# A one-hot tile built by four Vector comparisons with a per-partition number instead of one comparison of two SBUF operands, beside a stream of GpSimd gathers

## The reference

```python
# twice (cgconv, then relu)
z = concat([x[dst], x[src]], -1)
m = sigmoid(z @ Wf + bf) * softplus(z @ Ws + bs)
x = x + segment_sum(m, dst)
# twice (gat_conv, then batch norm)
alpha = leaky_relu(a_src[src] + a_dst[dst] + a_edge)
p = exp(alpha - segment_max(alpha, dst)[dst]);  p = p / segment_sum(p, dst)[dst]
out = segment_sum((x @ W)[src] * p[:, None], dst) + bias
```

## Time and profile before

| what | value |
|---|---|
| median of 3 runs | 11049.12 us (11041.77 to 11055.13) |
| profiled execution, span from the first to the last instruction | 9392.2 us |
| profiled execution, its own time | not given; the median of the runs is 1656.9 us above the span |
| GpSimd busy | 6571.9 us, 70% of the span |
| TensorE busy (weight loads) | 5120.9 us, 55% (4302.7 us, 46%) |
| Vector busy | 4670.8 us, 50% |
| ScalarE busy | 3046.4 us, 32% |
| gathers L677, L1134 | 3328 each, 985 and 961 ns mean |

### The profile page before, as it was taken

One profiled execution on the slowest core, in us unless ns is written; L12 is line 12 of the kernel. 1 busy time (PEld: TensorE's weight loads), 2 busy tenths in 40 slices (PEclk: granted clock), 3 DMA queues, 4 the chain that ended last, 5 costly groups with the idle time before them and its releaser, 6 DMA issues. The chain is left out here.

```text
span 9392.2 us, 131283 instructions
## 1 busy us (share of the span) xinstructions
PE 5120.9 (55%) x26955; PEld 4302.7 (46%) x26956; DVE 4670.8 (50%) x14160; ACT 3046.4 (32%) x8219; POOL 6571.9 (70%) x6801
## 2 busy tenths in 40 slices
PE   2677777777677777777533253434552234343444
PEld 1555555555555555555423243434542234343443
DVE  6555555555555555555623353434552235353546
ACT  0444444444444444444302122222320122121222
POOL 2777777777577777777557777777716777777771
PEclk6888787788778887887655555555555555555555
DMA  4322223222222232222232232222203223222221
GB/s 134 91 76 77 76 75 76 75 77 77 82 77 77 75 76 77 77 75 76 68 76 53 45 59 50 56 52 52 49 11 75 45 49 59 46 58 49 58 44 30
DMA packets 436755, 612.92 MB, mean 65 GB/s; under 512 B 180134, under 2 KB 217754, under 8 KB 434779
## 3 DMA queue, kind: packets, MB, share of 16 engines
q0 software_dynamic: 214032, 332.71, 17.2%
q1 hardware_dynamic: 217116, 262.20, 10.3%
q10 hardware_dynamic: 5193, 13.44, 0.4%
HBM read 575.04 MB, written 32.78 MB: 65 GB/s over the span
## 5 line engine op out<-in xcount | busy, mean ns | idle before, releaser
L677 POOL DMA_INDIRECT big<-q_table,idx_stage x3328 | 3279.5, 985 | 1007.8 <-issue 930.3
L1134 POOL DMA_INDIRECT big<-xl_table,idx_stage x3328 | 3199.1, 961 | 1007.9 <-issue 985.3
L1405 PE MATMUL bank<-msg,onehot 128*128 128x66 f32 x6656 | 1597.3, 424 | 2227.4 <-DVE wide L1265 2003.0
L1405 PEld LDWEIGHTS bank<-msg,onehot 128*128 128x128 f32 x6656 | 1480.8, 328 | 2276.9 <-issue 2186.1
L774 PE MATMUL bank<-big,ident 128*128 128x512 f32 x1664 | 1216.8, 821 | 1236.0 <-DMA big<-q_table,idx_stage 1145.6
L777 PEld LDWEIGHTS bank<-big,wide 128*128 128x128 f32 x6656 | 1217.7, 257 | 574.9 <-issue 574.9
L777 PE MATMUL bank<-big,wide 128*128 x6656 | 1208.0, 342 | 0.0
L577 DVE TENSOR_TENSOR onehot<-iota,dst_rel 128x512 f32<-128x512 f32 x1664 | 1145.7, 689 | 2.9 <-issue 2.9
L705 DVE SCALAR_TENSOR_TENSOR work<-bank,work 128x256 f32<-128x256 f32 x832 | 352.3, 423 | 1459.7 <-ACT work L747 1456.2
L742 ACT ACTIVATE work<-bank 128x512 f32<-128x512 f32 x832 | 496.2, 596 | 1783.4 <-PE bank L777 1781.1
L1265 DVE TENSOR_TENSOR wide<-wide,bank 128x66 f32 x3328 | 739.4, 222 | 553.8 <-issue 182.6
(11 more groups left out here) (216 smaller groups left out, 4138.3 us busy)
## 6 DMA issues: line engine op xcount, KB each, us to landing
wide<-rel_rows SPq DMA_DIRECT2D x416, 256.0 KB, 3.4
big<-rel_rows SPq DMA_DIRECT2D x416, 256.0 KB
big<-q_table,idx_stage POOLq DMA_INDIRECT x3328
big<-xl_table,idx_stage POOLq DMA_INDIRECT x3328
q_table<-wide SPq DMA_DIRECT2D x12, 1024.0 KB, 5.2
edge_rows<-big SPq DMA_DIRECT2D x25, 257.0 KB, 6.6
xl_table<-big SPq DMA_DIRECT2D x12, 520.0 KB, 6.7
big<-in_edge_attr ACTq DMA_DIRECT2D x6, 1024.0 KB
```

The source lines that it names most:

```text
L677: pool.indirect_dma_start(out=ring[:, u, s % GROUP, :], out_offset=None, in_=k.q_table, in_offset=bass.IndirectOffsetOnAxis(ap=k.idx_stage ...
L1134: pool.indirect_dma_start(out=buf[p][:, s, :], out_offset=None, in_=k.xl_table, in_offset=bass.IndirectOffsetOnAxis(ap=k.idx_stage[:, s:s ...
L1405: last_one = nc.tensor.matmul(sum_bank[c % UNROLL][:, i * P:i * P + C + 2], k.onehot[:, c % UNROLL, i, :], k.msg[:, c % UNROLL, i, 0:C + 2 ...
```

## The change

`build_onehot` writes the same tile. Before, one `tensor_tensor` compares `iota`, repeated four times, with the four numbers of `dst_rel`, each repeated 128 times: 512 elements per partition and two inputs in SBUF. After, four `tensor_scalar` write one step's 128 columns each: one input in SBUF (`iota`) and one [P, 1] scalar per instruction, a column of `dst_rel`. The last of the four increments the semaphore. Both callers keep their place for it.

```diff
 def build_onehot(nc, k, to, s):
 
-    return nc.vector.tensor_tensor(to, k.iota[:, :].unsqueeze(1).broadcast_to([P, GROUP, P]),
-                                   k.dst_rel[:, ds(s, GROUP)].unsqueeze(2).broadcast_to([P, GROUP, P]), ALU.is_equal)
+    for i in range(GROUP):
+        last_one = nc.vector.tensor_scalar(to[:, i, :], k.iota[:, :], k.dst_rel[:, ds(s + i, 1)], None, ALU.is_equal)
+    return last_one
```

## The result

The changed kernel takes 11205.17 us (median of 4 runs, 11199.27 to 11209.2), the kernel before beside it 11045.44 us (4 runs): ratio 1.0144, 95% interval 1.0130 to 1.0158. The forecast was 11011 us and its range ended at 11085. It is slower, by 160 us, where 38 us less were forecast.

What follows compares the result with a forecast made beforehand. GpSimd's 6656 gathers at 1.25 us were taken as the bound, 8320 of 9392 us. Terms -55 (stretch), +16 and +1 (where no gather hides Vector) gave -38: 11049 to 11011 us, range 10955 to 11085.

Steps and rivals of the forecast that it cites:

- If it isn't, it still costs nothing beside gathers: Vector's queue: three more address instructions per group are taken as covered, and otherwise still cost nothing while gathers run.
- no row says what fills it, and I take it as unchanged: Outside the profiled span: the 1657 us between span and median of the runs were taken to stay the same.
- GpSimd never waits for a buffer: GpSimd in the passes: its idle time is nearly all 'issue', so 6656 gathers at 1.25 us set 8320 us.
- wrong in its root: Stated failure condition: stretched gathers end elsewhere than 0.82 us after a comparison's end, or the time outside the span moves.
- stretch by one-hots: Gathers starting inside a one-hot comparison: their stretch falls from 122 to 67 us, a gain of 55 us.
- from the last gather of both attention passes on: After the attention passes' last gathers: Vector's queue sets the pace, 80 groups at 0.20 us more, +16 us.
- the 67 us that were to be left: Gathers beside the four new comparisons: remaining stretch, 10 ns per comparison, 40 ns per group, 67 us in all.
- So each comparison delays only gathers that start in its first 0.286 - 0.125 = 0.161 us: New one-hot comparisons: gathers starting in that window are delayed by 0.08 us on average, 10 ns per comparison.
- The turn within the four: Within a group's four comparisons: a gather goes on at the end of the comparison in which it starts.
- the first rival: Gathers beside the four comparisons get no turn within them: one 0.886 us hold, +195 us, 11244 us; chance 8%, half case 5%.
- Two-port stalls of the writing: Rival, gathers: a two-port comparison also stalls GpSimd's descriptor writing, 11864 us; chance 3%.
- No hold at all: Rival, gathers: the new comparison doesn't hold GpSimd but lasts some 0.335 us, -88 us, 10961 us; chance 10%.

Runs made afterwards that it cites:

- e5: The changed kernel measured again, unaltered, against the kernel before at the upper level: ratio 1.0140.
- e6: The changed kernel with its four comparisons always reading columns 0 to 3 of dst_rel, so no computed addresses, against the kernel before, upper level: 1.0026.
- e16: The changed kernel with dst_rel columns first copied to a small tile and read at fixed places, values kept, against the kernel before, upper level: 1.0042.
- e17: The changed kernel unaltered, measured beside the version with copied columns, against the kernel before at the upper level: 1.0142.
- e7: The kernel before with its one comparison always reading columns 0 to 3 of dst_rel, against the kernel before, upper level: 0.9987.
- e4: The kernel before plus three 128x2 tensor_scalar per group reading a fixed column, against the kernel before, upper level: 1.0064.
- e1: The kernel before, unaltered, profiled once more at the upper level: ratio 0.9994 to the kernel before.
- e12: The changed kernel unaltered, against the kernel before at the lower level: ratio 0.9911.
- e13: The changed kernel with each of its four comparisons as a 128x128 tensor_tensor, against the kernel before, lower level: 0.9943.
- e9: The kernel before with SyncE's rel_rows transfers in the loops filling 16 of 128 partitions, against the kernel before, lower level: 0.9992.
- e8: The kernel before with one comparison of 1024 elements building the one-hots of two groups, against the kernel before, upper level: 1.0030.
- e11: The kernel before with each batch's dst_rel columns copied once to a fixed tile in the attention passes, against the kernel before, lower level: 0.9989.
- e3: The kernel before plus three 128x2 tensor_scalar per group, each with its own computed dst_rel address, against the kernel before, upper level: 1.0110.
- e14: The kernel before plus three 128x2 tensor_scalar per group with computed addresses, against the kernel before, lower level: 1.0160.

## Why the prediction was wrong

**The step that failed at the upper level: "If it isn't, it still costs nothing beside gathers".** It said that the queue's three more address instructions per group either hide or cost nothing, since the gathers set the time. The trace that it was read from had them at 53 to 89 ns. In the runs that were timed many take 0.7 us, single one-hots take several microseconds in place of 0.9, and the gathers wait for buffers. The addresses cost 118 us by the medians of e5 and e6, and again 118 us by those of e16 and e17 (11098.39 - 10980.5; 1.00% by the ratios). The profiled executions say where, in us:

| compared | first passes | attention passes | after their last gathers |
|---|---|---|---|
| addresses: e5 less e6 | +4 | +98 | +14 |
| addresses: e17 less e16 | +28 | +88 | +19 |
| the change without them: e6 less e7 | +10 | +14 | +22 |
| three small instructions: e4 less e1 | +6 | +10 | +47 |

So the slow addresses cost little in the first passes, though most of the new slow entries lie there, and most of their price is in the attention passes, where ScalarE frees the gathers' buffers later. That slow entries delay the release of these buffers is what the waits suggest; it wasn't followed from entry to buffer. The next 0.3 to 0.4% (e6, e16) is loss beside the addresses, about half of it in e6 after the last gathers. More instructions alone cost there as well: e4 loses 0.64%, mostly after the last gathers, and not by longer holds (its gathers are busy for 14 us less than those of e1).

**The step under it: "no row says what fills it, and I take it as unchanged".** The profiled span was 1657 us below the median of the runs, and the prediction read this as time outside the span. It was a warning that the trace showed another level than the times. With it the whole argument "GpSimd never waits for a buffer" held for an execution of the lower level only. It was also the condition named for being wrong in its root.

**The term of the gain at the upper level.** The holds did fall: the gathers are busy 174 us less in e17 than in e1. But GpSimd idles 286 us more before them, waiting for buffers. A gain at the bound counts only while it is the bound.

**At the lower level, for which the sum was in fact made, the signs were right and one size was off.** The sum was -38 us, 0.4% of the span; measured, 0.9911, -83 us. By terms:

| term | forecast | e12 against the earlier trace rows |
|---|---|---|
| stretch by one-hots | -55 | -99 (122 to 24 us) |
| all of the gathers' busy time | -55 | -82 |
| from the last gather of both attention passes on | +16 | 213.1 to 222.3 and 213.9 to 220.6: +16 |
| sum | -38 | -62 by the spans, -83 by the medians |

(The profiled execution of e12 was the slowest of its four, 9331.96 us, which is why the two sums differ. Gathers take 947 ns in the median instead of 945, some 13 us in all, which gives back part of the 99.)

The mis-sized term is the 67 us that were to be left; 24 are. The number of gathers that start inside a comparison is not why (1014 in e12). If each were held to the comparison's end, as the prediction has it, their starts would give 74 us. What failed is "So each comparison delays only gathers that start in its first 0.286 - 0.125 = 0.161 us": it takes every gather in these 0.161 us as held. Those that start at their very beginning aren't, in the kernel before
```profile
500.86 0.75 DVE L577 TENSOR_TENSOR onehot<-iota,dst_rel 128x512 f32<-128x512 f32 x1
500.89 0.94 POOL L677 DMA_INDIRECT big<-q_table,idx_stage  x1 [0.30 <-issue]
```
nor in e12:
```profile
346.13 0.30 DVE L578 TENSOR_SCALAR onehot<-iota,dst_rel 128x128 f32<-128x128 f32 x1
346.17 0.94 POOL L678 DMA_INDIRECT big<-q_table,idx_stage  x1 [0.30 <-issue]
```
Counted over the traces, for gathers with more than 0.15 us of the comparison to go:

| the gather starts after the comparison's start by | before, tensor_tensor 128x512 | e13, tensor_tensor 128x128 | e12, tensor_scalar 128x128 |
|---|---|---|---|
| less than 50 ns | 0 of 59 held below 30 ns, 6 of 11 from 30 to 40 ns | 92 of 286 held | 3 of 255 held |
| 50 to 90 ns | all held (449 of 449 from 40 ns on) | 154 of 154 held | 186 of 327 held |
| 90 ns or more | all held | 177 of 177 held | 91 of 95 held |

Of the 74 us, 36 fall on the first 50 ns and 33 on 50 to 90 ns. In a hold of 0.69 us a few tens of ns at the start matter little; in one of 0.28 us they are most of what was left. It is also where tensor_scalar differs from tensor_tensor: 24 us against 42. Why its first 50 ns or more are free was not tested.

**What was right.** The end 0.82 us after the comparison in which the gather starts: all 253 that are stretched by over 20 ns in the first passes of the execution of the earlier trace rows, 438 of 439 in e1's first passes, and 286 of 343 in e12. The turn within the four, which leaves the first rival (+195 us) without ground: the longest stretch of any gather that starts inside a comparison of e12 is 0.26 us. The burst of four in 0.87 us (forecast 0.886) and 2.33 us per group after the last gather (9183.86 - 9181.53; forecast 2.34, before 2.14 by the earlier trace rows), at both levels. The comparison's duration: 281 ns median for 286; the means of 294 to 303 are within the 0.32 named. Vector's extra time is hidden at the lower level: idle time before the gathers is unchanged.

**The rivals.** Two-port stalls of the writing (+815 us, the reading of the Trainium skill's "SBUF — State Buffer", section "Who interferes with whom"): no run shows them; tensor_scalar gains more than tensor_tensor (0.9911 and 0.9943), and gathers take 0.947 us in the median. Whether the new comparison runs in such a mode at all, no run says: it takes 281 ns where the tensor_tensor of this size takes 284. (The 588 gathers beside L698 that the prediction names aren't found again: L698 alone begins inside 377, overlaps them for 115 us and stretches them by 1.1 us, which says the same.) "No hold at all" (-88 us) came near in size but not in kind: holds are there, short ones. The case that came, that the price of a queue entry isn't the same in every execution, was not among the rivals.

**What stays open.** What puts runs at the upper or the lower level, and what makes the queue entries slow there. Nothing in the kernels does: the same kernels met both. The load of transfers was to be tested by e9 and wasn't. And why the change still loses 0.3 to 0.4% at the upper level with its addresses gone.

## What to carry to other kernels

Compare the span of the profiled execution with the timed runs first; when they differ by more than a few microseconds, the trace shows other conditions than the times, and no wait that is missing in it may be taken as absent. Count the entries of each queue as well as its instructions: splitting one instruction into four with their own computed addresses costs nothing where an entry takes 57 ns and 1% where stretches of 0.7 us entries occur; copying the columns to a fixed place took that 1% back. A GpSimd gather is held by the Vector instruction that runs when it starts, if that one has been running for some tens of ns, so shorter comparisons give it its turn sooner (-0.9% here), as long as the gathers are what sets the time.

## What the runs showed of the hardware that was not expected

- Two levels, 9390 and 10940 to 11050 us for one kernel, 16 to 18% apart, and both on one chip (e5 to e8 and e9 to e11). The granted clock of the stretch 3000:4000 is 0.81 in the earlier trace rows and 0.75 in the one shown above, where TensorE has less to do.
- At the upper level, stretches in which a queue entry takes 0.6 to 0.8 us in place of some 0.05, in the queues of Vector, TensorE and SyncE and not in those of ScalarE and GpSimd; all but 5 of the 3321 in the changed kernel's Vector queue lie between the first and the last gather of a pass.
- A gather that starts within 30 ns after a 128x512 tensor_tensor isn't held by it (0 of 59), nor one within 50 ns after a 128x128 tensor_scalar (3 of 255 held). The comparison pays a little: 740 ns in the median beside such a gather, where it takes 685.
- Four tensor_scalar of 128x128 take 0.87 us and four tensor_tensor 0.89 us after the last gather (medians 281 and 284 ns each): for this size the second SBUF input costs no time on Vector, and the [P, 1] scalar saves none. A comparison of 128x2 still takes 236 to 245 ns in the mean (e3, e4, e14).
